# A filter for the top 16 by a threshold mask, attention values by a folded weight, and a third score buffer

## The reference

```
xn = layernorm(x)
# attention: three contexts, gated per token, one output product
gates = sigmoid(xn @ Wg + bg); gates /= gates.sum(-1) + 1e-6
comp  = attend(blocks of 4 tokens @ Wc + bc)      # 128 rows, padded with zeros to 512
sel   = attend(the 64 tokens with the best xn @ Ws + bs)   # 64 rows, padded to 512
win   = attend(windows of 32 tokens, step 16), its first 512 rows
s = concat(comp * g0, sel * g1, win * g2) @ Wo + bo
s = layernorm(0.5 * s + 0.5 * xn)
# experts: product keys, 8 heads
q = xn @ Wq.T ; sim = q . keys                    # 2 x 8 vectors of 32 scores per token
sx, sy = top_k(sim[0], 16), top_k(sim[1], 16)
scores, idx = top_k(sx[:, None] + sy[None, :], 16)
f = sum_k gelu(xn . W_down[idx]) * softmax(scores) * W_up[idx]
out = x + s * silu(f)
```

## Time and profile before

| | |
|---|---|
| Median of 3 runs | 284.59 us |
| The profiled execution's own time | 284.64 us |
| Its span, first to last instruction | 282.8 us |
| TensorE: matmuls (modelled ends), 1574 | 242.3 us busy, 86% |
| ScalarE, 1047 | 236.1 us busy, 83% |
| GpSimd, 342 | 224.1 us busy, 79% |
| VectorE, 2580 | 269.3 us busy, 95% |
| Share of VectorE in the chain that ended last | 62% |

### The profile page before, as it was taken

How to read it: one execution, slowest core, us unless ns; L and a number is a source line. 1 busy time by engine, 2 the same in 40 slices (tenths; PEclk the granted TensorE clock), 3 DMA queues, 4 the chain that set the end, 5 groups by cost and what they waited for, 6 DMA issues and landing times.

```text
span 282.8 us, 7961 instructions
## 1 busy us (share of the span) xinstructions
PE 242.3 (86%) x1574; PEld 176.7 (62%) x1574; DVE 269.3 (95%) x2580; ACT 236.1 (83%) x1047; POOL 224.1 (79%) x342
## 2 busy tenths in 40 slices
PE   7899797887988798989898889888888888889991
PEld 7566243575866675766576657666666666667780
DVE  5799999979999999999999999999999999999885
ACT  2465768589898999899989999999999999996943
POOL 7888610388688879997999799988998899888852
PEclk9999999797999999999999999999999999999997
DMA  7920000000000000100010001000010001000102
GB/s 174 279 71 2 0 1 0 2 1 0 5 1 0 5 0 3 39 1 3 1 38 3 1 0 38 7 0 5 10 31 2 0 1 41 2 1 3 37 3 74
DMA packets 11235, 6.29 MB, mean 22 GB/s; under 512 B 1457, under 2 KB 10674, under 8 KB 11186
## 3 DMA queue, kind: packets, MB, share of 16 engines
q1 hardware_dynamic: 9858, 5.12, 6.8%
q10 hardware_dynamic: 1328, 0.66, 1.1%
HBM read 3.67 MB, written 2.10 MB: 20 GB/s over the span
## 4 chain that ended last, share of the span: by engine, by line
DVE 62%; PE 14%; issue 8%; POOL 7%; ACT 6%; DMA 2%; ACTq 0%; POOLq 0%; DVEq 0%
DVE rest L1141 24%; DVE top L1130 13%; DVE top L1150 13%; DVE last L1174 6%; PE s_bank L1493 2%; DMA fwq_sb<-in_L_ffn_Wq 2%; POOL squareT L493 2%; DVE slot_gap L1159 2%; PE sim L1507 2%; PE f_bank L1500 1%; PE t_bank L1456 1%; PE c_bank L1500 1%; PE scratch L1487 1%; PE t_bank L1525 1%; POOL wgt L506 1%
## 5 line engine op out<-in xcount | busy, mean ns | idle before, releaser
L1141 DVE MATCH_REPLACE8 rest<-top,sim 128x32 f32<-128x32 f32 x512 | 85.8, 179 | 0.1
L1150 DVE MAX8 top<-rest 128x8 f32<-128x32 f32 x512 | 53.5, 177 | 0.7
L821 ACT ACTIVATE prob<-drop 128x50 f32<-128x50 f32 x224 | 51.6, 256 | 0.0
L1130 DVE MAX8 top<-sim 128x8 f32<-128x32 f32 x496 | 50.9, 178 | 0.6 <-PE sim L1507 0.6
L821 ACT ACTIVATION_READ_ACCUMULATOR prob<-drop 128x1 f32 x224 | 47.1, 214 | 0.0
L493 POOL TENSOR_TENSOR squareT<-sideT 100x512 bf16<-100x512 bf16 x31 | 32.5, 1048 | 15.2 <-ACT sideT L735 15.2
L1141 DVE MATCH_VALUE_LOAD rest<-top,sim 128x8 f32 x512 | 40.8, 80 | 0.3
L478 POOL TENSOR_TENSOR past<-gap,last 128x400 f32<-128x400 f32 x31 | 26.8, 864 | 11.2 <-DVE last L1174 11.2
L1507 PE MATMUL sim<-sim_w,xT_all 128*128 128x512 f32 x64 | 34.5, 621 | 0.8 <-ACT xT_all L771 0.8
L506 POOL TENSOR_TENSOR wgt<-prob,rden 128x400 f32<-128x400 f32 x30 | 25.6, 855 | 8.2 <-DVE rden L1120 8.2
L500 POOL TENSOR_TENSOR drop<-gap,out_by 128x400 f32<-128x400 f32 x30 | 31.0, 1034 | 0.9 <-ACT out_by L724 0.9
(11 more groups left out here) (289 smaller groups left out, 724.0 us busy)
## 6 DMA issues: line engine op xcount, KB each, us to landing
out<-y_sb SPq DMA_DIRECT2D x7, 256.0 KB, 2.3
x_sb<-in_L_attn_hidden_states SPq DMA_DIRECT2D x2, 256.0 KB, 4.0
fwq_sb<-in_L_ffn_Wq ACTq DMA_DIRECT2D x2, 256.0 KB, 6.0
x_sb<-in_L_attn_hidden_states SPq DMA_DIRECT2D x1, 512.0 KB, 5.4
wc_sb<-in_L_attn_Wc SPq DMA_DIRECT2D x1, 256.0 KB
out<-last_y SPq DMA_DIRECT2D x2, 128.0 KB, 1.9
wo_in<-in_L_attn_Wo SPq DMA_DIRECT2D x1, 192.0 KB
keys_sb<-in_L_ffn_keys ACTq DMA_DIRECT2D x1, 128.0 KB, 3.4
```

Of the source, the lines that this page charges most:

```text
L821: last = nc.scalar.activation(prob[d][:, h, :], drop[:, h, :], ACT.Exp, scale=-1.0, accum_out=den[d][:, h:h + 1])
L1130: last = nc.vector.max(top[d][:, v, 0:8], sim_bank[d][:, bass.ts(v, KEYS)])
L1141: last = nc.vector.match_replace(out=rest[:, v, :], in_to_replace=top[d][:, v, 0:8], in_values=sim_bank[d][:, bass.ts(v, KEYS)], imm_value ...
L1150: last = nc.vector.max(top[n % 2][:, v, 8:16], rest[:, v, :])
```

## The change

Five edits, in one diff:

1. The strikes are gone. `mark_above` compares all 512 scores with each vector's eighth value and writes a bf16 mask; `strike_above` adds -1e38 where the mask is set and writes `rest`; `sum_above` counts the mask per vector; `spill_above` and `put_ties` turn that count into 8 extra columns of `rest` that hold the eighth value once for each score marked beyond eight (a tie), and a very low number otherwise. `next_8` now reads 40 columns a vector.
2. The order on VectorE is new: `first_8(n + 1)` is done in turn n, in two halves between the steps of tile n, and the last gaps come at the end of a turn. `top` has three buffers; `scores(n + 2)` is issued in turn n, in most turns behind `expert_weights(n - 4)`, and waits for `put_ties(n)`. `scores(4)` stands before `hidden(4)`, `scores(5)` before `project_blocks(0)`.
3. Wv times Wo is made once (`turn_values`, `fold_values`, copies to `wvT`, `bvo`, `wvo`), so `project_values`, the product and copy of `vw`, and `vcs` are gone.
4. bv times Wo becomes three rows of `vww`, and the window probabilities get three gate columns, copied by GpSimd for each batch; `WROWS` is `WKEYS + 3`. Twelve small DMAs put the rows there.
5. The residual is a product of the identity with two tiles of `xn_all` at once.

```diff
@@ VectorE
-            def first_8(n):
+            def first_8(n, halves=range(2)):
-                if n >= 2:
-                    dve.wait_ge(topT_ready, n - 1)
+                if n >= 3:
+                    dve.wait_ge(topT_ready, n - 2)
                 dve.wait_ge(sim_ready, n + 1)
...
-                for v in range(q * VECS // 4, (q + 1) * VECS // 4):
-                    last = nc.vector.match_replace(out=rest[:, v, :], in_to_replace=top[d][:, v, 0:8],
-                                                   in_values=sim_bank[d][:, bass.ts(v, KEYS)],
-                                                   imm_value=NO_SCORE)
+            def mark_above(n):
+                dve.wait_ge(sim_top8, n + 1)
+                if n >= 1:
+                    dve.wait_ge(summed_above, n)
+                nc.vector.tensor_tensor(above[:, :, :], sim_bank[n % 2][:, :].rearrange("p (v k) -> p v k", k=KEYS),
+                                        eighth(n, KEYS), ALU.is_ge).then_inc(above_done, 1)
+            def strike_above(n):
+                dve.wait_ge(above_done, n + 1)
+                if n >= 1:
+                    dve.wait_ge(top_done, 2 * n)
+                nc.vector.scalar_tensor_tensor(rest[:, :, 0:KEYS], above[:, :, :], STRUCK,
+                                               sim_bank[n % 2][:, :].rearrange("p (v k) -> p v k", k=KEYS),
+                                               ALU.mult, ALU.add).then_inc(struck, 1)
+            def sum_above(n):
+                dve.wait_ge(struck, n + 1)
+                nc.vector.tensor_reduce(sim_bank[n % 2][:, 0:TIES], above[:, :, :], AX_X, ALU.add
+                                        ).then_inc(summed_above, 1)
+            def spill_above(n):
+                dve.wait_ge(summed_above, n + 1)
+                nc.vector.scalar_tensor_tensor(tie_slots(n),
+                                               sim_bank[n % 2][:, 0:TIES].unsqueeze(2).to_broadcast([P, VECS, 8]), 2.0,
+                                               rank_row[:, 7:15].unsqueeze(1).to_broadcast([P, VECS, 8]),
+                                               ALU.mult, ALU.subtract).then_inc(spill_done, 1)
+            def put_ties(n):
+                dve.wait_ge(spill_done, n + 1)
+                nc.vector.scalar_tensor_tensor(rest[:, :, KEYS:KEYS + 8], tie_slots(n), SPILL, eighth(n, 8),
+                                               ALU.mult, ALU.min).then_inc(sim_used, 1)
@@ VectorE, select_tokens: one batch of gaps inside
+                    if r == 2:
+                        gaps_of_pairs(n - 2)
+                        gaps_of_thirds(n - 2)
+                        last_gaps(n - 2)
@@ VectorE, the end of first_turns, after tile 2
+                select_tokens(3)
+                invert_gates()
+                mark_above(3)
+                strike_above(3)
+                first_8(4)
+                sum_above(3)
+                spill_above(3)
+                put_ties(3)
+                mark_above(4)
+                gaps_of_pairs(2)
+                next_8(3, 0)
+                gaps_of_thirds(2)
+                last_gaps(2)
+                next_8(3, 1)
+                invert_gate_sums()
@@ VectorE, turn(n)
+                strike_above(n)
+                if n + 1 in tiles:
+                    first_8(n + 1, [0])
+                sum_above(n)
+                invert_sums(n - 4)
+                spill_above(n)
+                if n + 1 in tiles:
+                    first_8(n + 1, [1])
+                put_ties(n)
                 if j == 0:
                     maxima(b - 1)
+                if n + 1 in tiles:
+                    mark_above(n + 1)
+                next_8(n, 0)
+                gaps_of_pairs(n - 1)
+                if j == 0:
                     inverse_row_sums(b - 1)
+                next_8(n, 1)
+                gaps_of_thirds(n - 1)
+                if n < TILES - 1:
                     last_gaps(n - 1)
@@ ScalarE, after take_topT(1)
+            act.wait_ge(values_in, 1)
+            nc.scalar.activation(wvT[:, :], f_bank[:, 0:D], ACT.Copy)
+            nc.scalar.activation(bvo[:, :, :], f_bank[0:1, D:4 * D].rearrange("p (r d) -> p r d", r=3),
+                                 ACT.Copy).then_inc(bvo_done, 1)
             side_of(0)
             take_gaps(1)
+            act.wait_ge(values_folded, 1)
+            nc.scalar.activation(wvo[:, :, :], f_bank[:, D:4 * D].rearrange("p (r d) -> p r d", r=3),
+                                 ACT.Copy).then_inc(wvo_done, 1)
@@ ScalarE, turns
-                    unit(b - 1, U_V, [(vcs[:, :], 0, bv_sb, 1.0)])
-                    unit(b, U_VW, [(vw[:, :], 0, bv_sb, 1.0)])
@@ GpSimd, scale_probs
+                nc.gpsimd.tensor_copy(p_win[:, :, WKEYS:WROWS],
+                                      gates[:, :, :, bass.ds(b, 1)].rearrange("p g t a -> p t (g a)"))
@@ TensorE, first part
-                    scores(2)
...
                 if b == 2:
+                    scores(2)
                     top_columns(0)
             product.then_inc(z_ready, 1)
+            scores(3)
+            turn_values()
             top_columns(1)
             pair_gaps(1)
-            scores(3)
+            fold_values()
             places_matrix()
             pe.wait_ge(count_in, 1)
             for b in range(B):
                 if b == 1:
                     transpose_gates()
+                    pe.wait_ge(wvo_done, 1)
+                if b == 4:
+                    scores(4)
                 hidden(b)
...
-            scores(4)
             transpose_masks()
-            project_window(0, U_VW, wv_sb)
             count_ranks()
             transpose_sides(1)
+            scores(5)
             project_blocks(0)
@@ TensorE, new functions and the values
+            def turn_values():
+                pe.wait_ge(w_late, 16 * LATE_DMAS)
+                pe.wait_ge(wo_step, 4)
+                nc.tensor.transpose(f_bank[:, 0:D], wv_sb[:, :], ident[:, :])
+                mm(f_bank[0:1, D:4 * D], bv_sb[:, 0:1], wo_sb[:, :, :].rearrange("p r d -> p (r d)"),
+                   start=True, stop=True).then_inc(values_in, 1)
+            def fold_values():
+                pe.wait_ge(bvo_done, 1)
+                mm(f_bank[:, D:4 * D], wvT[:, :], wo_sb[:, :, :].rearrange("p r d -> p (r d)"),
+                   start=True, stop=True).then_inc(values_folded, 1)
...
-                    last = mm(o[0:WKEYS, bass.ts(g, D)], vw[:, k0:k0 + WKEYS], wo_sb[:, WIN, :], start=True, stop=True)
+                    last = mm(o[0:WKEYS, bass.ts(g, D)], xT_all[:, k0:k0 + WKEYS], wvo[:, WIN, :], start=True, stop=True)
@@ TensorE, attention_out
-                        mm(o, xT_all[:, bass.ts(b * TB + j, P)], off_mean[:, :], start=True, stop=False)
+                        if j % LAST == 0:
+                            mm(out_bank[:, bass.ds(j * D, LAST * D)], ident[:, :],
+                               xn_all[:, bass.ds(b * TB + j, LAST), :].rearrange("p t d -> p (t d)"),
+                               start=True, stop=False)
@@ TensorE, turn(n): scores, in every turn
-                    scores(n + 1)
+                    if n + 2 in tiles:
+                        scores(n + 2)
```

More of the change, by code:

```diff
@@ L196, in program @@
         qw = sb("qw", [P, L])
-        kw, vw = (sb(n, [P, WTOK]) for n in ("kw", "vw"))
+        kw = sb("kw", [P, WTOK])
         csT = sb("csT", [P, CS])
-        qcs, kcs, vcs = (sb(n, [P, CS]) for n in ("qcs", "kcs", "vcs"))
-        vww = sb("vww", [WKEYS + 1, TB, D])
+        qcs, kcs = (sb(n, [P, CS]) for n in ("qcs", "kcs"))
+        vww = sb("vww", [WROWS + 1, TB, D])
         vwc = sb("vwc", [P, 2, D])
@@ L213, in program @@
         s_norm = [sb(f"s_norm{i}", [P, TB, D]) for i in range(2)]
-        top = [sb(f"top{i}", [P, VECS, TOPK]) for i in range(2)]
-        rest = sb("rest", [P, VECS, KEYS])
+        top = [sb(f"top{i}", [P, VECS, TOPK]) for i in range(3)]
+        above = sb("above", [P, VECS, KEYS], BF16)
+        rest = sb("rest", [P, VECS, KEYS + 8])
         topT = sb("topT", [P, 2 * P])
@@ L1033, in _ @@
             out_by_of(TILES - 3)
-            unit(B - 1, U_V, [(vcs[:, :], 0, bv_sb, 1.0)])
             take_gaps(TILES - 1)
@@ L1314, in _ @@
-            for n in range(TB):
-                first_turn(n)
+            first_turns()
             for n in range(TB, TILES):
@@ L1661, in transpose_window_probs @@
                 for g in range(TB):
-                    last = nc.tensor.transpose(o[0:WKEYS, bass.ts(g, P)], p_win[:, g, :], ident[:, :])
+                    last = nc.tensor.transpose(o[0:WROWS, bass.ts(g, P)], p_win[:, g, :], ident[:, :])
                 last.then_inc(unit_full, 1)
@@ L1737, in turn @@
                     pair_gaps(n - 1)
-                    scores(n + 1)
                     expert_weights(n - 4)
-                    project_window(b, U_VW, wv_sb)
+                    if n + 2 in tiles:
+                        scores(n + 2)
                     count_places(n - 2)
@@ L1747, in turn @@
```

(4 more changed lines are left out.)

212 lines of the change are left out of this document (89 added, 123 removed).

## The result

| | before | after |
|---|---|---|
| median of the runs | 283.92 us (283.16 to 284.63, 4 runs) | 292.96 us (291.12 to 295.75, 4 runs) |
| profiled execution, its span, mean granted clock | 284.64, 282.8, 0.982 | 291.12, 289.1, 0.978 |
| M of the first batch | 62.50 | 69.07 |
| the next six batches | 173.19 (28.87 each) | 173.47 (29.22, then 28.81 to 28.97) |
| from the last of these M to the end of the span | 47.1 | 46.6 |

A forecast was written before the change was run, and what follows sets the result against it. VectorE was taken to set the pace, with ScalarE 1.5 us behind and taking back most savings; first part +4.4, batches -1.95, tail -0.5 on 284.64 us gave 286.6, stated as 286.5, range 281.0 to 290.0.

The forecast's parts named there:

- The filter's price: VectorE's work per tile in the new filter: 6.65 us, with mark, strike and sum at 0.60 each.
- The rival with passes of 0.70: VectorE's mark, strike and sum cost 0.70 or more each, not 0.60; 290.2 us in all; chance 0.13.
- VectorE as the bound: Rival for steady batches: VectorE alone sets the pace, six batches save 8.6 us, total 279.9; chance 0.15.
- a hidden first part: Rival: TensorE's added products fall into waits, first batch's maxima end at most 1 us later, total 283.1; chance 0.12.
- ScalarE takes it back: Steady batches: VectorE waits for ScalarE's gap copies and exps, so a batch takes 28.6 us, not VectorE's own 27.43.
- The first batch: First of the six batches: no expert output for ScalarE to copy, only 0.84 us lost, so 28.3 us.
- The first part: Start to the end of the first batch's maxima: 66.9 instead of 62.50, +4.4 us (+3.4 to +5.3).
- the gate chain: First part, work ahead of the gate reciprocal: 2.8 us longer, 1.05 from the fold's products; add_one ends near 53.4.
- the second chain: First part: scores(5) waits for put_ties(3) at 58.2, ahead of project_blocks(0) on TensorE; first batch's maxima end at 66.5.
- the clock: First part: TensorE, idle some 3 us before 58.2, may fall to its lower 1.2 GHz level, costing 1.3 us more.
- The tail: After the last batch: -0.5 us (0 to -2), the last maxima still hanging on TensorE's block scores.
- the stand of 3.5 us: First part: VectorE stands idle for some 3.5 us before the gate reciprocal, which starts near 53.4.

The follow-up runs named there:

- e12_three_steady: Changed kernel with invert_gates behind put_ties(3), maxima(b - 1) behind spill_above, take_gaps ahead of window_exps, window key product behind pair_gaps; 280.2 us, ratio 0.988.
- e2_gates_late: Changed kernel with only invert_gates() moved on VectorE, from behind select_tokens(3) to behind put_ties(3); 287.1 us, ratio 1.011 to the kernel before.
- e13_fold_alone: Kernel before with only the folded values, gate columns and merged residual, strikes and order of scores kept; 284.9 us, ratio 1.004.
- e3_keep_clock: Changed kernel with four unused 512-column products on TensorE ahead of scores(5), order unchanged; 291.9 us.
- e11_gates_two_steady: Changed kernel with invert_gates behind put_ties(3), maxima(b - 1) behind spill_above, take_gaps ahead of window_exps; 282.7 us, ratio 0.993 to the kernel before.

## Why the prediction was wrong, step by step

**The filter's price: right.** 6.64 for a tile against 6.65, wide passes 0.59 to 0.60, MAX8 over 40 columns 0.81 for 8 against 0.83. The rival with passes of 0.70 is refuted; so are the other two, VectorE as the bound (batches are 28.8, not 27.5) and a hidden first part (M_0 is 6.6 later, not 1). The Trainium skill's figure for PSUM, page "VectorE: DVE Perf Modes", section "The TRN2 errata", 120 cycles plus the columns, makes mark and strike 0.66 each (an estimate from it). What they cost here from start to start is less, 0.60 and 0.59. As an instruction's own duration 0.67 does stand in the rows, near that figure, but the next one starts 0.07 or 0.08 before its end.

**ScalarE takes it back: right in kind, short by 0.23 a batch.** VectorE waits where I said, 0.39, 0.28 and 0.52 (predicted 0.46, 0.38, 0.33). The term that failed is the end of the gap copy with j=2: I took ScalarE's 15.9 us as fixed, since it had no wait in it. It got one, of 0.2 us, because I gave the moved `scores` and the rest of TensorE's new order nothing. A stretch without waits bounds from below only; each of its inputs must be followed into the new order too. `e12_three_steady` showed that a product ahead of `attention_out` made it late.

**The first batch: wrong.** I said 28.3, since ScalarE has no expert output to copy there. It took 29.22, and 28.82 in `e2_gates_late`, where M_0 doesn't come late. In this batch ScalarE waits for TensorE ahead of the same gap copy, 0.75 for the top columns and 0.50 for the attention rows: the work that is missing is replaced by waiting for what comes in anyway. The other 0.4 is ScalarE's side copy, which overlaps M_0 in the changed kernel and starts the exps late. With the 0.25 of each of the other five (28.85 against 28.6), this is the 2.2 us between -1.95 and +0.3.

**The first part: right in kind, 2.2 us short.** Three terms. The fold's products count 1.8 in the gate chain, not 1.05 (`e13_fold_alone`): the wait for the top copy that I let 0.45 of them fall into moved along with them and shrank only from 0.66 to 0.47. With this the gate reciprocal is at 54.32, not 53.4. From there both chains run as written: VectorE's own work 12.6 against 12.5, and `put_ties(3)` at 59.17, 1.0 late, carries the second chain to 67.5 instead of 66.5. (The terms listed for that chain add up to 65.1 for the start of the maxima and not to the 65.7 given; the rows bear the 65.7 out, so 0.6 of hand-overs from one instruction to the next is missing in the list.) Last, the clock. I priced it at 1.3 for the second chain and put less than half of that into the forecast, as a hedge between 65.9 and 67.8. The clock did fall, and it is worth 1.8 there by the products of `e3_keep_clock`: 67.5 with this is 69.3, measured 69.07. Between `e11_gates_two_steady` and `e12_three_steady` it is worth 2.8 for the whole stretch. My reason for it, TensorE's idle time before `scores(5)`, isn't borne out: the level had fallen at 55.26, before that time began.

**The tail: right**, -0.55 against -0.5, with the wait for the block scores where it was expected.

**The range: too narrow above.** The measured median is 6.5 above my 286.5: 2.2 from the first part, 2.2 from the batches, and the rest mostly the 1.8 between the profiled execution and the median. The range ended at 290, from one case with the lower clock in one place. (At the low end of that case my own terms add up to 283.5 and not to 284.4.) The runs of the changed kernel differ by their mean clock (0.978 to 0.961 goes with 291.1 to 295.8). The kernel before was steadier: 283.1 to 285.4 in 23 runs. The change gives TensorE less work and its clock is lower in more runs; that the one comes from the other isn't shown. I had priced the clock as a term of 1.3 us and not as a spread of several.

**What caused the slowdown.** The gate reciprocal stands ahead of the filter of tile 3 on VectorE. Moving it takes the ratio to before from 1.029 to 1.011 (`e2_gates_late`), about 5 of some 8 us. At an equal clock the position is worth 2.7 us at M_0 (`e12_three_steady`), and the rest of the gain goes with a clock that stays at its upper level more often; why it does so isn't shown. I had seen the stand of 3.5 us and priced it, and did not ask whether it was needed.

## What to carry to other kernels

When an engine that paces the kernel gets less work, look first at what it will wait for in its own program order: a small instruction with a late input costs its whole lateness to everything behind it, and may be moved at no cost. In a loop over two engines only the work on the loop counts; here moving maxima 1 us forward gave 0.95 us a batch and the saved 1.2 us of VectorE's work gave none. A delay is worth what the next wait doesn't absorb: the same 1.8 us met a later wait of 1.84 in one kernel and a standing VectorE in the other. And products put in to keep the clock up have to end before the work behind them is ready, at the lower level too.

## What the hardware showed

Two kernels with the same program up to M_0 had granted clocks of 1.00 and of 0.53, 0.50 and 0.69 from 54 to 66, and differed by 2.8 us. The busy share of TensorE ahead of it was alike (2.37 of 4 us from 50 to 54, and 3.31 of 4 from 46 to 50, in both), so from these windows it can't be read which of the two comes.

Filling TensorE's idle time with products that nobody reads brought the clock to 0.97 for the four us in which it had been 0.50; the slice before it, from 54 to 58, stayed low at 0.60, and the first of these products ran in it.

The lower level doesn't double every product. From start to start, `scores(5)` takes 0.86 at the upper level (`e3_keep_clock`, 60.34 to 61.20) and 1.84 at the lower (changed kernel, 59.31 to 61.15), but the eight products for the blocks take 1.80 and 1.83 (61.20 to 63.00, 61.15 to 62.98).

A sum over a bf16 mask of 512 columns takes 0.59 from start to start, as the passes over f32: the halved width bought nothing. MAX8 over 40 columns of `rest` in SBUF costs 0.101 each, over 32 columns of scores in PSUM 0.099 (0.79 for 8); before, over 32 columns of `rest`, it was 0.094 (0.75 for 8, 137.29 to 138.04). From the same source the 8 columns more thus cost 0.007, predicted 0.009.
